# Splitting the first group's loads between SyncE's and ScalarE's DMA queues, and moving the constants and weights behind ScalarE's half

## The chip, the cores and the metric

The kernel runs on one core of one Trainium2 chip. The metric is device time in microseconds (us) from start to end of one execution; lower is better. A core has TensorE (PE, the matrix engine), VectorE (DVE), ScalarE (ACT), GpSimd (POOL) and SyncE (SP, which here only issues transfers), and 16 DMA engines that all its transfers share. An engine issues a transfer by an instruction of its own; a transfer adds 16 to a semaphore when it has landed.

## The reference

`x` is (32, 128, 56, 56) in float32. It is normalised over groups of 4 channels, whitened over groups of 8 channels with the inverse square root of their covariance, scaled, shifted and added back.

```python
def _zca_forward(x, weight, bias, groups=16):      # N, C, H, W = x.shape, c = C // groups
    xc = xf - mu                                    # per channel, over N*H*W
    xg = xc.reshape(G, c, M)
    cov = jnp.einsum('gim,gjm->gij', xg, xg) / M + EPS * jnp.eye(c)
    e, v = jnp.linalg.eigh(cov)
    proj = jnp.einsum('gik,gk,gjk->gij', v, jax.lax.rsqrt(e), v)
    xw = jnp.einsum('gij,gjm->gim', proj, xg).reshape(C, M)
    return xw * weight + bias                       # back in N, C, H, W
out = x + _zca_forward(_gn(x), L0_conv_weight, L0_conv_bias)
```

## The kernel before

**Tiling.** The 128 channels are 16 groups of 8. A group `g` of all 32 samples is two tiles (`s` = 0, 1) of 128 partitions (16 samples by 8 channels) by 3136 pixels, 1.6 MB each. Tiles live in `ring`, which holds 7 groups. A tile is loaded in two halves (`q`) of 1568 pixels, each half by four transfers of 32 partitions, 196 KB each: 16 transfers a group. `x_landed[g % 7][s][q]` counts the four of a half.

**Order.** Every engine walks the same loop of ticks (64 a group) and does what tables such as `BN_AT` say is due in that tick, for several groups in turn; the order on an engine is fixed, and semaphores join the engines. The loads of groups 1 to 6 stand before SP's loop; those of groups 7 and up wait for the store of the group that had their place.

**A group's way.** DVE takes statistics of each tile in seven chunks of 448 pixels (`row_stats`, L338): chunk 0 waits for half 0 and chunk 3 for half 1. After the 14th chunk come `rows` (L344), matmuls with constants from `cst` and small DVE steps (`deviations`, `var_eps`, `scales`, `centre`, L349 to L385), which yield `y_mul` and `y_add`. POOL and ACT then normalise the tile in pieces (L314, L499), split each into a high and a low half-precision part (ACT L511, POOL L322), DVE transposes them (L395) and PE sums their products (`ps_gram`). A chain of small matrix products gives the inverse root, and PE applies it (`ps_apply`), ACT writes the result over the tile (L520) and SP stores it.

**Start.** SP issues the 16 transfers of group 0 (tile 0 half 0, tile 0 half 1, tile 1 half 0, tile 1 half 1), then three transfers on `const_landed`: `cst` (128 x 760 floats, 380 KB) and the two rows of `wb8`, weight and bias, each gathered as 8 x 16 single floats, then groups 1 to 6. PE's first work waits for all three (`const_landed` at 48): a matmul that spreads the weights over 128 partitions (`wb_product`). DVE reads it in `read_weights` (L451 to L455), which in its fixed order stands after the 14 chunks of group 0 and ahead of `rows(0)` and of everything later. In names of the profile `wb8` and `wb` are both `wb`.

Of the kernel before, what the change touches and what calls it, by code (L numbers as in the profile page):

```python
# [15 lines left out]
CG = 8  # L16
GROUPS = C // CG
GN = 4
TILES = N * CG // P
# [6 lines left out]
RING = 7  # L26
# [19 lines left out]
PAIRS = CG // 2  # L46
HALVES = 2
HALF = HW // HALVES
# [87 lines left out]
def zca_residual(nc: bass.Bass, x: bass.AP, weight: bass.AP, bias: bass.AP, const: bass.AP, out: bass.AP):  # L136
    with ExitStack() as ctx:
        def sb(name, shape, dt=F32):
            return ctx.enter_context(nc.sbuf_tensor(name, shape, dt))
# [4 lines left out]
        def sem(name):  # L144
            return ctx.enter_context(nc.semaphore(name))

        ring = sb("ring", [P, RING, TILES, HW])
        hl_ring = sb("hl_ring", [P, HL_RING, PIECE_MAX, 2], F16)
        t_ring = sb("t_ring", [P, T_RING, PIECE_MAX, 2], F16)
        cst = sb("cst", [P, CONST_COLS])  # L150
        wb8 = sb("wb8", [CG, 2, GROUPS])
# [33 lines left out]
        x_landed = [[[sem(f"x_landed_{r}_{s}_{q}") for q in range(HALVES)] for s in range(TILES)]  # L185
                    for r in range(RING)]
        out_stored = [[sem(f"out_stored_{r}_{s}") for s in range(TILES)] for r in range(RING)]
        const_landed = sem("const_landed")
# [23 lines left out]
        x_dram = x.rearrange("(s n) (g c) h w -> g s n c (h w)", s=TILES, c=CG)  # L212
# [30 lines left out]
        def span(p):  # L243

            s, q = divmod(p, len(PIECE_UNITS))
            lo, hi = PIECE_UNITS[q]
            return s, slice(lo * UNIT, hi * UNIT)

        def width(p):
            lo, hi = PIECE_UNITS[p % len(PIECE_UNITS)]  # L250
            return (hi - lo) * UNIT
# [5 lines left out]
        def due(places, t):  # L257

            items = places.items() if isinstance(places, dict) else enumerate(places)
            return [((t - a) // TICKS, k) for k, a in items  # L260
                    if (t - a) % TICKS == 0 and 0 <= (t - a) // TICKS < GROUPS]

        def due_one(place, t):
            return [g for g, _ in due([place], t)]

        ticks = range(FIRST_TICK, LAST_TICK + 1)
        block = ctx.enter_context(nc.Block())

        @block.sync
        def _(sp):  # L270
            def load(g, s):
                r = g % RING
                if g >= RING:
                    sp.wait_ge(out_stored[r][s], 16 * PAIRS * (g // RING))
                for q in range(HALVES):
                    px = slice(q * HALF, (q + 1) * HALF)
                    for a in range(PAIRS):
                        sp.dma_start(ring[a::PAIRS, r, s, px], x_dram[g, s][:, a::PAIRS, px]).then_inc(  # L278
                            x_landed[r][s][q], 16)

            def store(g, s):
                r = g % RING
                sp.wait_ge(out_ready, PARTS * g + PARTS // TILES * (s + 1))
                for a in range(PAIRS):
                    sp.dma_start(out_dram[g, s][:, a::PAIRS, :], ring[a::PAIRS, r, s, :]).then_inc(
                        out_stored[r][s], 16)

            for s in range(TILES):
                load(0, s)
            sp.dma_start(cst[:], const).then_inc(const_landed, 16)  # L290
            with nc.allow_non_contiguous_dma(reason="256 channel scalars, once"):
                sp.dma_start(wb8[:, 0, :], weight.rearrange("(g j) o -> j (g o)", j=CG)).then_inc(const_landed, 16)
                sp.dma_start(wb8[:, 1, :], bias.rearrange("(g j) o -> j (g o)", j=CG)).then_inc(const_landed, 16)
            for g in range(1, RING):
                for s in range(TILES):
                    load(g, s)
            for t in ticks:
                for g, s in due(LOAD_AT, t):
                    if g >= RING:
                        load(g, s)  # L300
                for g, s in due(STORE_AT, t):
                    store(g, s)
            for r in range(RING):
                for s in range(TILES):
                    sp.wait_ge(out_stored[r][s], 16 * PAIRS * len(range(r, GROUPS, RING)))
# [182 lines left out]
        @block.scalar  # L488
        def _(act):
            def stats_root(g):  # L490
                act.wait_ge(stat_step, STAT_OPS * g + VAREPS)
                nc.scalar.activation(root[:], vareps, ACT.Sqrt).then_inc(root_done, 1)  # L492

            def normalise(g, p):
                s, px = span(p)
                act.wait_ge(stat_step, STAT_OPS * g + Y_SET)
                y = ring[:, g % RING, s, px]
                i = g % STAT_RING
                nc.scalar.activation(y, y, ACT.Identity, bias=y_add[:, i, s:s + 1],  # L499
                                     scale=y_mul[:, i, s:s + 1]).then_inc(y_act_ready, 1)  # L500

            def high_part(g, p):
                s, px = span(p)
                i = PIECES * g + p
                if p in Y_POOL:
                    act.wait_ge(y_pool_ready, len(Y_POOL) * g + sorted(Y_POOL).index(p) + 1)
                else:
                    act.wait_ge(y_act_ready, len(Y_ACT) * g + sorted(Y_ACT).index(p) + 1)
                if i >= HL_RING:
                    act.wait_ge(t_ready, i - HL_RING + 1)  # L510
                nc.scalar.copy(hl_ring[:, i % HL_RING, 0:width(p), 1], ring[:, g % RING, s, px]).then_inc(h_ready, 1)  # L511

            def finish(g, u):
                s, q = divmod(u, PARTS // TILES)
                if u == 0:
                    act.wait_ge(stat_step, STAT_OPS * (g + 1))
                i = PARTS * g + u
                act.wait_ge(applied, i + 1)
                px = slice(2 * BANK * q, 2 * BANK * (q + 1))
                nc.scalar.activation(ring[:, g % RING, s, px].rearrange("p (a b) -> p a b", a=2),  # L520
                                     ps_apply[:, i % 2 * 2:i % 2 * 2 + 2, 0:BANK],
                                     ACT.Identity, bias=fin_add[:, g % STAT_RING, s:s + 1],
                                     scale=scale[:, g % STAT_RING, s:s + 1]).then_inc(out_ready, 1)

            def read_hop(g, k):
                e = g % 2

                def copy(dst, src):
                    act.wait_ge(solve_mm[e], HOPS * (g // 2) + k + 1)
                    nc.scalar.copy(dst, src).then_inc(solve_read[e], 1)  # L530

                if k in HOP_WV[:-1]:
                    copy(wv[:, e], s_wv[e])
                if k == HOP_WV[-1]:
                    copy(zz[:, e], s_z[e])
                if k == HOP_T:
                    copy(tz[:, e], s_t[e])
                if k == HOP_V:
                    act.wait_ge(res_copied, g + 1)
                    copy(zx[:, e], s_zx[e])  # L540

            for t in ticks:
                for g, k in due(HOP_READ_AT, t):
                    read_hop(g, k)
                for g in due_one(ROOT_AT, t):
                    stats_root(g)
                for g, u in due(FINISH_AT, t):
                    finish(g, u)
                for g, p in due(Y_ACT, t):
                    normalise(g, p)  # L550
                for g, p in due(H_AT, t):
                    high_part(g, p)
# [122 lines left out]
```

## Time and profile before

| | |
|---|---|
| median of 3 runs | 403.22 us (402.53 to 403.56) |
| profiled execution | 402.31 us |
| its span, first to last instruction | 400.5 us |
| TensorE granted clock, mean | 0.994 |
| busy PE / DVE / ACT / POOL | 85% / 79% / 78% / 72% |
| moved by DMA | 103.72 MB, mean 259 GB/s |

The span is 1.8 us shorter than the time of the same execution; what lies around it is not in the trace. A row of the timeline gives the start, the length, the engine, line, operation and names, and how long the engine was idle before it and what ended that. A row of DMA issues gives the time in which the issuing engine was busy with them, not that of the transfer. PEld is PE's weight load.

### The profile page before, as it was taken

The page shows a single profiled execution, that of the slowest core. Times are in us where ns is not written, and L with a number is a line of the kernel's source. Part 1 is how long each engine was busy: PE and PEld are TensorE (multiplying, and loading weights), DVE is VectorE, ACT ScalarE, POOL GpSimd, SP SyncE. Part 2 cuts the span into 40 slices and gives each one's busy share as a digit, 9 for nine tenths or more (in the row PEclk, how much of TensorE's full clock was granted, in tenths as well). Part 3 has the DMA queues.
Part 4 walks back from the last instruction along what each step waited for, and adds up shares of the span by engine and source line. Part 5 has one row for each costly group of instructions (what it writes and reads, how often), then busy time and mean ns, then how long its engine had stood idle before and what let it go on. Part 6 is the DMA issues. An engine that isn't in the chain of part 4 may idle for free.

```text
span 400.5 us, 8571 instructions
## 1 busy us (share of the span) xinstructions
PE 339.3 (85%) x3202; PEld 214.2 (53%) x3202; DVE 314.5 (79%) x869; ACT 313.8 (78%) x449; POOL 287.9 (72%) x148
## 2 busy tenths in 40 slices
PE   0114366999999999999999999999999999998891
PEld 0013345666656566656565666565656666554450
DVE  2679999899999999999999999999999984531100
ACT  1065565689999999999999999898989898954572
POOL 0059979978888888889898888888888888820000
PEclk9999999999999999999999999999999999999997
DMA  7999999923999999999999999988993535354667
GB/s 224 278 305 293 295 285 291 291 50 142 292 318 314 320 306 313 304 298 316 313 300 297 297 309 315 301 281 292 319 321 121 181 118 180 124 200 160 211 204 279
DMA packets 18890, 103.72 MB, mean 259 GB/s; under 512 B 6432, under 2 KB 6432, under 8 KB 14752
## 3 DMA queue, kind: packets, MB, share of 16 engines
q1 hardware_dynamic: 18848, 103.18, 80.3%
q8 instruction: 25, 0.41, 0.4%
q14 instruction: 17, 0.14, 0.1%
HBM read 51.77 MB, written 51.38 MB: 258 GB/s over the span
## 4 chain that ended last, share of the span: by engine, by line
PE 80%; DVE 8%; POOL 4%; SPq 3%; issue 2%; ACT 1%; DMA 1%; DVEq 0%
PE ps_apply L557 48%; PE ps_small L557 15%; PE ps_gram L557 13%; PE ps_stat L557 4%; POOL hl_ring L322 3%; DVE bn L338 3%; DVE t_ring L395 3%; SPq L278 2%; DMA wb<-in_L_conv_bias_dram 1%; DVE spread_in L405 1%; ACT tz L530 1%; POOL ring L314 1%; DVE pp L424 0%; ACT hl_ring L511 0%; ACT ring L520 0%
## 5 line engine op out<-in xcount | busy, mean ns | idle before, releaser
L322 POOL TENSOR_TENSOR hl_ring<-ring,hl_ring 128x1024 f16<-128x1024 f32 (+1 forms) x96 | 230.8, 2415 | 41.2 <-ACT hl_ring L511 41.2
L557 PE MATMUL ps_apply<-ring,a_t 128*128 128x392 f32 x512 | 202.2, 520 | 0.0
L520 ACT ACTIVATE ring<-ps_apply,fin_add,scale 128x784 f32<-128x784 f32 x128 | 127.4, 995 | 16.6 <-PE ps_apply L557 16.5
L338 DVE BATCH_NORM_STATS2 bn<-ring 128x6 f32<-128x448 f32 x224 | 128.9, 602 | 8.8 <-DMA ring<-in_x_dram 8.8
L511 ACT CAST hl_ring<-ring 128x1024 f16<-128x1024 f32 (+1 forms) x96 | 129.1, 1371 | 6.7 <-POOL ring L314 3.6
L395 DVE STREAM_TRANSPOSE t_ring<-hl_ring 128x1024 f32<-128x1024 f32 (+1 forms) x96 | 119.2, 1242 | 2.9 <-POOL hl_ring L322 2.8
L557 PEld LDWEIGHTS ps_apply<-ring,a_t 128*128 128x128 f32 x512 | 87.3, 190 | 43.3 <-ACT ring L520 2.7
L557 PE MATMUL ps_gram<-t_ring 128*128 128x64 f16 x1568 | 68.5, 200 | 10.8 <-DVE t_ring L395 10.8
L314 POOL TENSOR_SCALAR ring<-ring,y_mul,y_add 128x1024 f32<-128x1024 f32 (+1 forms) x48 | 57.9, 1212 | 23.5 <-DVE y_add L382 23.5
L499 ACT ACTIVATE ring<-ring,y_add,y_mul 128x1024 f32<-128x1024 f32 (+1 forms) x48 | 59.9, 1249 | 7.9 <-DVE y_add L382 7.9
L557 PEld LDWEIGHTS ps_gram<-t_ring 128*128 128x128 f16 x1568 | 58.2, 102 | 14.0 <-DVE t_ring L395 11.3
L424 DVE SCALAR_TENSOR_TENSOR pp<-ps_small,cst 16x16 f32<-16x16 f32 x112 | 17.2, 154 | 39.3 <-PE ps_small L557 38.0
L557 PEld LDWEIGHTS ps_small<-wv 16*16 16x16 f32 x224 | 12.0, 90 | 46.6 <-issue 35.2
L530 ACT COPY wv<-ps_small 16x32 f32<-16x32 f32 x112 | 18.2, 163 | 17.5 <-PE ps_small L557 17.3
L557 PE MATMUL ps_small<-pp,wv 16*16 16x16 f32 (+1 forms) x224 | 23.5, 178 | 3.0 <-DVE pp L424 3.0
L557 PE MATMUL ps_small<-wv 16*16 16x16 f32 x224 | 23.7, 179 | 2.3 <-ACT wv L530 2.3
L557 PE MATMUL ps_small<-wv,pp 16*16 16x16 f32 x192 | 18.9, 172 | 0.0
L492 ACT ACTIVATE root<-ps_stat 128x2 f32<-128x2 f32 x16 | 2.4, 150 | 19.4 <-DVE ps_stat L360 19.3
L557 PEld LDWEIGHTS ps_small<-pp,wv 16*16 16x16 f32 (+1 forms) x224 | 11.8, 89 | 9.3 <-DVE pp L424 4.1
L557 PEld LDWEIGHTS ps_stat<-dr,cst 128*128 128x128 f32 x64 | 10.6, 216 | 8.8 <-DVE dr L377 5.2
L557 PE MATMUL ps_small<-wb,cst 8*128 8x32 f32 x2 | 0.6, 407 | 17.0 <-DMA wb<-in_L_conv_bias_dram 17.0
L557 PE MATMUL ps_stat<-dr,cst 128*128 128x1 f32 x64 | 9.6, 253 | 4.8 <-DVE dr L377 4.8
(59 smaller groups left out, 199.7 us busy)
## 6 DMA issues: line engine op xcount, KB each, us to landing
ring<-in_x_dram SPq DMA_DIRECT2D x256, 196.0 KB, 4.3
out_dram<-ring SPq DMA_DIRECT2D x128, 392.0 KB, 4.9
cst<-const_dram SPq DMA_DIRECT2D x1, 380.0 KB
wb<-in_L_conv_weight_dram SPq DMA_DIRECT2D x1, 0.5 KB
wb<-in_L_conv_bias_dram SPq DMA_DIRECT2D x1, 0.5 KB
```

The source lines that it names most:

```text
L278: sp.dma_start(ring[a::PAIRS, r, s, px], x_dram[g, s][:, a::PAIRS, px]).then_inc(x_landed[r][s][q], 16)
L314: nc.gpsimd.tensor_scalar(y, y, y_mul[:, i, s:s + 1], y_add[:, i, s:s + 1], ALU.mult, ALU.add).then_inc(y_pool_ready, 1)
L322: nc.gpsimd.tensor_tensor(hl[:, :, 0], ring[:, g % RING, s, px], hl[:, :, 1], ALU.subtract).then_inc(l_ready, 1)
L338: nc.vector.bn_stats(bn[:, g % 2, s, c, :], ring[:, g % RING, s, c * BN:(c + 1) * BN]).then_inc(bn_done, 1)
L395: nc.vector.transpose(words(t_ring[:, i % T_RING, 0:n]), words(hl_ring[:, i % HL_RING, 0:n])).then_inc(t_ready, 1)
L405: nc.vector.tensor_scalar(spread_in[:, g % 2, s], id8w[:, g], y_mul[:, g % STAT_RING, s:s + 1], None, ALU.mult)
L424: nc.vector.scalar_tensor_tensor(out=pp[:, e], in0=s_m[e], scalar=POLY[it][1], in1=ai[:, CW * it:CW * (it + 1)], op0=ALU.mult, op1=ALU.add ...
L499: nc.scalar.activation(y, y, ACT.Identity, bias=y_add[:, i, s:s + 1], scale=y_mul[:, i, s:s + 1]).then_inc(y_act_ready, 1)
L511: nc.scalar.copy(hl_ring[:, i % HL_RING, 0:width(p), 1], ring[:, g % RING, s, px]).then_inc(h_ready, 1)
L520: nc.scalar.activation(ring[:, g % RING, s, px].rearrange("p (a b) -> p a b", a=2), ps_apply[:, i % 2 * 2:i % 2 * 2 + 2, 0:BANK], ACT.Iden ...
L530: nc.scalar.copy(dst, src).then_inc(solve_read[e], 1)
L557: return nc.tensor.matmul(out_, lhsT, rhs, start=start, stop=stop, skip_group_check=True)
```

## The change

A helper `half_load` issues the four transfers of one half of a tile on the engine that it is given. `load` uses it, so that groups 1 and up are issued as before. For group 0, SP now issues half 0 of both tiles, and goes on with group 1. ACT, ahead of its loop, issues half 1 of both tiles, then `cst`, weight and bias. Semaphores, destinations and waits are the same.

```diff
+        def half_load(engine, g, s, q):
+            px = slice(q * HALF, (q + 1) * HALF)
+            for a in range(PAIRS):
+                engine.dma_start(ring[a::PAIRS, g % RING, s, px], x_dram[g, s][:, a::PAIRS, px]).then_inc(
+                    x_landed[g % RING][s][q], 16)
...
             for s in range(TILES):
-                load(0, s)
-            sp.dma_start(cst[:], const).then_inc(const_landed, 16)
-            with nc.allow_non_contiguous_dma(reason="256 channel scalars, once"):
-                sp.dma_start(wb8[:, 0, :], weight.rearrange("(g j) o -> j (g o)", j=CG)).then_inc(const_landed, 16)
-                sp.dma_start(wb8[:, 1, :], bias.rearrange("(g j) o -> j (g o)", j=CG)).then_inc(const_landed, 16)
+                half_load(sp, 0, s, 0)
             for g in range(1, RING):
...
+            for s in range(TILES):
+                half_load(act, 0, s, 1)
+            act.dma_start(cst[:], const).then_inc(const_landed, 16)
+            with nc.allow_non_contiguous_dma(reason="256 channel scalars, once"):
+                act.dma_start(wb8[:, 0, :], weight.rearrange("(g j) o -> j (g o)", j=CG)).then_inc(const_landed, 16)
+                act.dma_start(wb8[:, 1, :], bias.rearrange("(g j) o -> j (g o)", j=CG)).then_inc(const_landed, 16)
             for t in ticks:
```

What SP issues at the start of the program, before (L278 is a transfer of `x`):

```order
L278 DMA ring<-in_x_dram 32x1x1568 x16
L290 DMA cst<-const_dram 128x760
L292 DMA wb<-in_L_conv_weight_dram 8x16x1
L293 DMA wb<-in_L_conv_bias_dram 8x16x1
L278 DMA ring<-in_x_dram 32x1x1568 x96
```

The same place on SP in the changed kernel, where a transfer of `x` is L269 and a store L288:

```order
L269 DMA ring<-in_x_dram 32x1x1568 x104
L288 DMA out_dram<-ring 16x2x3136 x8
L269 DMA ring<-in_x_dram 32x1x1568 x8
L288 DMA out_dram<-ring 16x2x3136 x4
L269 DMA ring<-in_x_dram 32x1x1568 x8
```

Eight of the first 16 transfers and the three small ones are gone from SP, so that the first of group 1 is its ninth.

ACT's first instructions before:

```order
L492 ACT_TABLE_LOAD
L492 ACTIVATE root<-ps_stat 128x2
L499 ACTIVATE ring<-ring,y_add,y_mul 128x1024
L511 CAST hl_ring<-ring 128x1088
L511 CAST hl_ring<-ring 128x1024 x2
```

ACT's first instructions in the changed kernel:

```order
L269 DMA ring<-in_x_dram 32x1x1568 x8
L543 DMA cst<-const_dram 128x760
L545 DMA wb<-in_L_conv_weight_dram 8x16x1
L546 DMA wb<-in_L_conv_bias_dram 8x16x1
L491 ACT_TABLE_LOAD
L491 ACTIVATE root<-ps_stat 128x2
L498 ACTIVATE ring<-ring,y_add,y_mul 128x1024
L510 CAST hl_ring<-ring 128x1088
```

The eleven transfers stand ahead of the table load, which was ACT's first instruction.

## Rows read from the trace of the kernel before

**Rows 1.** The page: the chain that ended last, shares of the span.
```profile
PE 80%; DVE 8%; POOL 4%; SPq 3%; issue 2%; ACT 1%; DMA 1%; DVEq 0%
PE ps_apply L557 48%; PE ps_small L557 15%; PE ps_gram L557 13%; PE ps_stat L557 4%; POOL hl_ring L322 3%; DVE bn L338 3%; DVE t_ring L395 3%; SPq L278 2%; DMA wb<-in_L_conv_bias_dram 1%; DVE spread_in L405 1%; ACT tz L530 1%; POOL ring L314 1%; DVE pp L424 0%; ACT hl_ring L511 0%; ACT ring L520 0%
```

**Rows 2.** The chain in order of time, first 20 us: start, length, what.
```profile
11.61 0.37 SPq L292
11.99 0.04 issue
12.03 4.92 DMA wb<-in_L_conv_bias_dram
16.94 0.04 issue
16.99 0.65 PE ps_small L557 x2
17.63 0.02 issue
17.66 0.17 DVE wb L451
```

**Rows 3.** Timeline of DVE, first 30 us.
```profile
6.08 1.68 DVE L338 BATCH_NORM_STATS2 bn<-ring 128x6 f32<-128x448 f32 x3 [5.12 <-DMA ring<-in_x_dram]
9.22 2.21 DVE L338 BATCH_NORM_STATS2 bn<-ring 128x6 f32<-128x448 f32 x4 [1.47 <-DMA ring<-in_x_dram]
11.82 1.68 DVE L338 BATCH_NORM_STATS2 bn<-ring 128x6 f32<-128x448 f32 x3 [0.40 <-DMA ring<-in_x_dram]
15.29 2.20 DVE L338 BATCH_NORM_STATS2 bn<-ring 128x6 f32<-128x448 f32 x4 [1.79 <-DMA ring<-in_x_dram]
17.66 0.17 DVE L451 TENSOR_SCALAR wb<-ps_small 128x16 f32<-128x16 f32 x1 [0.16 <-PE ps_small L557]
...
19.90 1.14 DVE L338 BATCH_NORM_STATS2 bn<-ring 128x6 f32<-128x448 f32 x2
```

**Rows 4.** Timeline of SP's queue, first 50 us.
```profile
0.74 10.20 SPq L278 DMA_DIRECT2D ring<-in_x_dram  x16
10.98 0.59 SPq L290 DMA_DIRECT2D cst<-const_dram  x1
11.61 0.37 SPq L292 DMA_DIRECT2D wb<-in_L_conv_weight_dram  x1
12.03 0.28 SPq L293 DMA_DIRECT2D wb<-in_L_conv_bias_dram  x1
12.35 37.51 SPq L278 DMA_DIRECT2D ring<-in_x_dram  x58
```

**Rows 5.** Windows: stretch and length, busy by engine (count), PEclk, DMA share, GB/s.
```profile
2.00:3.00 1.00, 0.00 (x0) 0.00 (x0) 0.00 (x0) 0.01 (x1) 0.00 (x0) 1.00 0.72 207
...
13.00:14.00 1.00, 0.00 (x0) 0.00 (x0) 0.50 (x1) 0.00 (x0) 0.00 (x0) 1.00 0.89 203
14.00:15.00 1.00, 0.00 (x0) 0.00 (x0) 0.00 (x0) 0.00 (x0) 0.00 (x0) 1.00 0.99 221
15.00:16.00 1.00, 0.00 (x0) 0.00 (x0) 0.71 (x2) 0.00 (x0) 0.00 (x0) 1.00 0.75 179
16.00:17.00 1.00, 0.01 (x1) 0.01 (x1) 1.00 (x3) 0.00 (x0) 0.00 (x0) 1.00 0.94 364
```

**Rows 6.** Windows of longer stretches, same columns.
```profile
18.00:28.00 10.00, 2.16 (x8) 1.93 (x8) 7.85 (x27) 4.22 (x5) 3.75 (x3) 1.00 1.03 304
28.00:60.00 32.00, 14.33 (x191) 12.30 (x191) 30.44 (x63) 19.35 (x21) 28.97 (x15) 1.00 1.03 292
...
80.00:100.00 20.00, 19.75 (x200) 12.52 (x199) 18.50 (x53) 18.57 (x27) 15.99 (x9) 1.00 0.30 97
```

**Rows 7.** The page: DMA packets of the whole run, and issues with KB each.
```profile
DMA packets 18890, 103.72 MB, mean 259 GB/s; under 512 B 6432, under 2 KB 6432, under 8 KB 14752
...
ring<-in_x_dram SPq DMA_DIRECT2D x256, 196.0 KB, 4.3
out_dram<-ring SPq DMA_DIRECT2D x128, 392.0 KB, 4.9
cst<-const_dram SPq DMA_DIRECT2D x1, 380.0 KB
wb<-in_L_conv_weight_dram SPq DMA_DIRECT2D x1, 0.5 KB
```

**Rows 8.** Timeline, first 45 us: ACT's first work.
```profile
0.73 1.28 ACT L492 ACT_TABLE_LOAD   x1 [0.73 <-PEq L660]
...
21.14 0.17 ACT L492 ACTIVATE root<-ps_stat 128x2 f32<-128x2 f32 x1 [19.13 <-DVE ps_stat L360]
```

**Rows 9.** Waits of the whole run: who waited for whom, us, times, longest.
```profile
DVE bn L338 <- DMA ring<-in_x_dram: 8.8, 4, 5.1
```

More of the change, by code:

```diff
@@ L275, in load @@
                 for q in range(HALVES):
[L276 to L279, printed above, removed]
+                    half_load(sp, g, s, q)
             def store(g, s):
```

## The prediction

> **What bounds the kernel now.** I read the chain of the page first: PE holds 80% of it, and at its head stand transfers issued by SP and the landing of the bias [rows 1]. The chain in order of time shows that head: SP issues until 12.03, the bias lands 4.92 us later at 16.94, PE spreads the weights, and DVE reads them at 17.66 [rows 2]. DVE's timeline shows how close a second chain runs: the four halves of group 0 are taken up at 6.08, 9.22, 11.82 and 15.29, the last four chunks take 2.20 us, and DVE then idles only 0.16 us for the weights [rows 3]. Two things therefore set 17.66: the 14 chunks, done at 17.49, and the bias at 16.94. Both must come earlier if anything is to be won, and either alone delays everything, because all later DVE work, group 1's chunks at 19.90 among it [rows 3], stands behind the reading of the weights.
>
> Is the stream of transfers or the issuing the limit at the start? SP takes 10.20 us for 16 issues, or 0.64 us each with the gap to the next [rows 4]. With a full backlog the core moves 304 GB/s [rows 6], so a transfer of 196 KB (200,704 bytes, [rows 7]) takes 0.66 us. The stream is the limit from the start, by a hair. Data flows at 207 GB/s in the first window, so it began about 2.3 [rows 5]. Sixteen transfers need 2.3 + 16 x 0.66 = 12.9. The first four land at 6.08 where 2.3 + 4 x 0.66 is 4.9, so landing lags by 1.1: the sixteenth could land at 14.0. It did at 15.29, in the stretch from 13 to 16, where only 203, 221 and 179 GB/s moved [rows 5]. That is where cst and the single floats of weight and bias go through.
>
> A shift at the head is a shift of the end. DVE waits for loads four times in all, 8.8 us [rows 9], and those are the four waits of group 0 [rows 3]; behind it DVE is busy 30.44 of 32 us, then PE 19.75 of 20 [rows 6]. No later wait for a load is there to absorb or give back time. I count one for one.
>
> **The change, part by part.**
>
> *Eight issues off SP.* Together SP and ACT issue group 0 by 0.74 + 8 x 0.64 = 5.9 instead of 10.98 [rows 4]. The stream does not go faster for it, since it was the limit. SP goes on with group 1 at 5.9, so two backlogs share the DMA engines from then on. If they alternate evenly, ACT's eighth transfer is the sixteenth served, and lands at 14.0.
>
> *Order of landing.* Both halves of tile 0 now fill together: half 0 is served seventh, half 1 eighth (2.3 + 8 x 0.66 + 1.1 = 8.7). Tile 1's half 0 is the fifteenth and lands at 13.3. DVE then has all seven chunks left, at 0.55 us each (2.20 / 4): 13.3 + 3.9 = 17.2, against 17.49. So the statistics gain 0.3 us at most; what was an overlap of chunks with the last half is given up. An uneven share, ACT's issues being slower, say, only moves the sixteenth later.
>
> *cst, weight and bias on ACT's queue.* They are issued at 5.9 to 7.2 instead of 10.98 to 12.3, but stand behind ACT's half and beside SP's backlog. Alone on the stream they took from 14.0 (the sixteenth's due landing) to 16.94: 2.9 us. New is what SP's queue sends between them. The trace has no second busy queue, so this price must be bounded. From below: ACT's small transfers are served at once, 0, and the bias lands at 14.0 + 2.9 = 16.9, as before. From above: each packet of theirs lets one whole packet of x pass.
>
> The page tells how many packets they are. 6432 packets are under 512 B [rows 7]: the 256 single floats, and 6176 others, which is 385 x 16 + 2 x 8: one completion for each engine and transfer, with weight and bias on 8 engines only. So on each of those 8 engines cst is 8 rows and a completion, and weight and bias are 16 floats and a completion each: 9 + 17 + 17 = 43 packets. A transfer of x is three packets an engine (2 rows of 6272 B, a completion) in 0.66 us, 0.22 us a packet on average. If the engines alternate packet by packet, 43 x 0.22 = 9.5 us go in between. The bias lands at 14.0 + 2.9 + 9.5 = 26.4. With 0.33 for each (only rows of x counted) it would be 14.2, and with cst shared by bytes and no turn for it, 34 x 0.22 = 7.5. I take 9.5, since the profile counts single floats and completions as packets of their own, and a packet is the nearest thing in the trace to a unit of turns.
>
> The Trainium skill's page "DMA: Bandwidth & Descriptors", section "Queues, rings and completion order", says that SP's and ACT's queues are two rings on each of the same engines, served in turn, a whole packet at a time, and that a packet typically holds 9 to 17 descriptors. No row here shows turns. If the 17 entries of weight on an engine were one such packet, the engine would go through them in one turn, which is the first rival below.
>
> *ACT.* Eleven issues at 0.64 and less put the table load from 0.73 to about 7.2, and its 1.28 us end by 8.5; ACT's first work is at 21.14 [rows 8]. Nothing else is queued there. Cost nothing; the cover is 12 us.
>
> *The sum.* DVE reads the weights at 26.4 + 0.7 (PE's matmuls and the hand-over, 16.94 to 17.66, [rows 2]) = 27.1 instead of 17.66: +9.5. The statistics, done by 17.2, wait. Against the profiled execution, 402.31 + 9.5 = 411.8; the median of the runs is 0.9 above that execution, so 412.7. A gain from group 1 having landed meanwhile isn't there: its chunks did not wait before.
>
> **The rivals.** Measurement of this kernel can tell about 0.3%, 1.2 us, from no change.
>
> *Turns of whole transfers, or order of arrival.* cst, weight and bias each let one transfer of x pass: 3 x 0.66 = 2.0. By arrival it is about the same, as SP has issued three of group 1 by the time that ACT has issued the bias. Bias at 18.9, +2.0, 405.2. For it: it is the simplest way for an engine to share, and the skill's packet of many descriptors gives it. Against it: the packets of the profile are single rows and floats.
>
> *No change.* Either ACT's small transfers are hardly held up, or the two issuers hold each other up so that SP gets no head start (issues at 1.3 us each, and the order of before in effect; the change would then not do what it says). DVE is bound by the chunks at 17.2 to 17.5: within 1.2 us of 403.2.
>
> *Faster.* Two queues on each engine lift the stream. For one microsecond after the dip it ran at 364 GB/s [rows 5]. At that rate a transfer takes 0.55: the sixteenth lands at 2.3 + 8.8 + 1.1 = 12.2, the fifteenth at 11.7, chunks end at 15.5, and the bias, if not held up, comes at 12.2 + 2.9 = 15.1 and is read at 15.8: -1.9, 401.3. It decides only if the bias lands before 15.7; with even one transfer of x let past for each of the three, it lands at 16.7 and nothing is won. Against it speaks the flat 304 and 292 GB/s with a deep backlog [rows 6]. The same page of the Trainium skill, section "Issuing engines are not separate DMA queues", says that issuing on several engines saves only issue time; the 304 GB/s agrees so far as one queue can show it.
>
> **How the numbers follow.** Packet-wise turns 0.45 (its own range 410 to 417, from 7.5 and 14.2); turns of whole transfers 0.30 (404.4 to 407); between these two or beyond by another sharing 0.05; no change 0.14; faster 0.06. The likeliest gives 412.7. From 404.3 to 416.0 the range leaves out no change, faster, and the far end of the first. Faster 0.06, same 0.14, slower 0.80.
>
> **What the profile after would show.** DVE's waits: both halves of tile 0 near 8.7 with one long wait, tile 1 near 13.3. If the step on the turns is right, PE's first matmul starts near 26.5 and DVE's L451 idles some 9 us, released by PE; with whole transfers it starts near 19. The windows from 14 to 26 should then stay near 300 GB/s without the dip. ACT's table load is near 7. Everything after L451 keeps its distances. The prediction is wrong if the first matmul starts before 17.5, if the halves of group 0 land much before 13, or if a later wait on POOL or PE swallows the delay.

## The result, and the profile after

The changed kernel takes 411.64 us (median of 4 runs, 409.7 to 414.2), the kernel before 403.12 (402.53 to 403.56): 1.0216 times as long, 95% interval 1.0154 to 1.0278. Slower, as forecast: the medians are 8.5 us apart, where 9.5 were forecast, and the whole interval lies above 1. The profiled execution took 412.55 us with a span of 410.7, 10.2 more than before. Its traffic is split over two queues now. From the page of the profile: queue and kind, then packets, MB and the share of the 16 engines' time.

```profile
q1 hardware_dynamic: 18048, 101.18, 75.2%
q10 hardware_dynamic: 800, 2.00, 1.7%
```

q10 is ACT's: 8 transfers of x, cst, weight and bias. The chain of the page names the new wait, against 1% in [rows 1]:

```profile
PE ps_apply L562 48%; PE ps_small L562 15%; PE ps_gram L562 12%; DMA wb<-in_L_conv_bias_dram 4%; PE ps_stat L562 4%; POOL hl_ring L321 3%; DVE bn L337 3%; DVE t_ring L394 3%; ACTq L269 1%; DVE spread_in L404 1%; ACT tz L529 1%; POOL ring L313 1%; DVE pp L423 0%; ACT hl_ring L510 0%; ACT ring L519 0%
```

In order of time, the same chain (before: [rows 2]):

```profile
5.99 0.60 ACTq L543
6.63 0.81 ACTq L545
7.47 17.38 DMA wb<-in_L_conv_bias_dram
24.90 0.65 PE ps_small L562 x2
25.57 0.18 DVE wb L450
```

The bias was issued at 7.47 instead of 12.03 and landed 17.4 us later instead of 4.9. The timeline shows both queues and DVE (before: [rows 3, 4, 8]):

```profile
0.74 34.77 SPq L269 DMA_DIRECT2D ring<-in_x_dram  x54
0.75 5.21 ACTq L269 DMA_DIRECT2D ring<-in_x_dram  x8
...
7.79 1.28 ACT L491 ACT_TABLE_LOAD   x1 [7.79 <-issue]
9.84 3.79 DVE L337 BATCH_NORM_STATS2 bn<-ring 128x6 f32<-128x448 f32 x7 [8.88 <-DMA ring<-in_x_dram]
14.67 3.79 DVE L337 BATCH_NORM_STATS2 bn<-ring 128x6 f32<-128x448 f32 x7 [1.05 <-DMA ring<-in_x_dram]
...
25.57 0.18 DVE L450 TENSOR_SCALAR wb<-ps_small 128x16 f32<-128x16 f32 x1 [7.11 <-PE ps_small L562]
```

The four waits for x became two, the chunks of a tile run in one piece of seven, and DVE, done with all 14 at 18.46, then stands still for 7.11 us. Meanwhile the stream is full, with x of group 1 and later (columns as in [rows 5]):

```profile
18.00:20.00 2.00, 0.00 (x0) 0.00 (x0) 0.46 (x1) 0.00 (x0) 0.00 (x0) 1.00 1.00 311
20.00:22.00 2.00, 0.00 (x0) 0.00 (x0) 0.00 (x0) 0.00 (x0) 0.00 (x0) 1.00 1.04 326
22.00:24.00 2.00, 0.00 (x0) 0.00 (x0) 0.00 (x0) 0.00 (x0) 0.00 (x0) 1.00 1.07 339
```

**Where the 10.2 us went.** L450 is 7.9 us late (25.57 against 17.66), and the first `ps_apply` matmul just as late: 83.57 against 75.64. The rest arises there. First the kernel before, then the changed one, PE's timeline:

```profile
75.64 2.98 PE L557 MATMUL ps_apply<-ring,a_t 128*128 128x392 f32 x4
...
79.20 1.58 PE L557 MATMUL ps_apply<-ring,a_t 128*128 128x392 f32 x4
```

```profile
83.57 2.98 PE L562 MATMUL ps_apply<-ring,a_t 128*128 128x392 f32 x4
...
87.37 2.98 PE L562 MATMUL ps_apply<-ring,a_t 128*128 128x392 f32 x4
...
91.39 1.58 PE L562 MATMUL ps_apply<-ring,a_t 128*128 128x392 f32 x4
```

Four matmuls take 2.98 us at first and 1.58 later, which I read as TensorE at the lower of its two clocks (1.2 GHz) and then at the higher (2.4 GHz); the section on the clock shows why. Before, one set of four ran at the lower clock, after, two. From the first `ps_apply` to the 33rd it was 22.0 us before and 23.9 after (22.02 and 23.85). From there to the last `ps_apply` the two kernels keep their distance to 0.1 us. So: 7.9 for the bias, 1.8 for the clock, 0.1 on the way, and 0.4 behind the last `ps_apply`. Those 0.4 are not the change's: the trace of before has 8.8 us there, and every other trace below, kernels with an early start among them, has 9.1 to 9.2.

### The profile page after: what moved, and what is told of

Its sections match the earlier page's. It is cut to its first block, busy times and chain, and to the rows that moved or that the text cites. A ratio compares the mean times of both kernels' runs of the same rounds, so it can differ in the third digit from the quotient of the medians.

```text
span 410.7 us, 8571 instructions
## 1 busy us (share of the span) xinstructions
PE 341.2 (83%) x3202; PEld 215.2 (52%) x3202; DVE 314.6 (77%) x869; ACT 313.7 (76%) x449; POOL 288.2 (70%) x148
## 4 chain that ended last, share of the span: by engine, by line
PE 78%; DVE 8%; DMA 4%; POOL 4%; ACTq 2%; issue 1%; ACT 1%; DVEq 0%
PE ps_apply L562 48%; PE ps_small L562 15%; PE ps_gram L562 12%; DMA wb<-in_L_conv_bias_dram 4%; PE ps_stat L562 4%; POOL hl_ring L321 3%; DVE bn L337 3%; DVE t_ring L394 3%; ACTq L269 1%; DVE spread_in L404 1%; ACT tz L529 1%; POOL ring L313 1%; DVE pp L423 0%; ACT hl_ring L510 0%; ACT ring L519 0%
## 5 line engine op out<-in xcount | busy, mean ns | idle before, releaser
L519 ACT ACTIVATE ring<-ps_apply,fin_add,scale 128x784 f32<-128x784 f32 x128 | 127.5, 996 | 16.5 <-PE ps_apply L562 16.4
L423 DVE SCALAR_TENSOR_TENSOR pp<-ps_small,cst 16x16 f32<-16x16 f32 x112 | 17.2, 154 | 40.9 <-PE ps_small L562 39.5
L562 PE MATMUL ps_small<-wb,cst 8*128 8x32 f32 x2 | 0.6, 407 | 24.9 <-DMA wb<-in_L_conv_bias_dram 24.9
```

The source lines that it names most:

```text
L423: nc.vector.scalar_tensor_tensor(out=pp[:, e], in0=s_m[e], scalar=POLY[it][1], in1=ai[:, CW * it:CW * (it + 1)], op0=ALU.mult, op1=ALU.add ...
L562: return nc.tensor.matmul(out_, lhsT, rhs, start=start, stop=stop, skip_group_check=True)
```

## The experiments

The kernel before was run beside them again: 404.56 (25 runs), 403.77 (16) and 404.55 (19) in three sessions, in a spread of some 402 to 405.7. Each kernel's ratio is against its own session. "L451" is DVE's reading of the weights, whatever its line in that kernel.

### The change once more

> The changed kernel once more, for a second trace. Packet-wise turns: PE's first matmul again starts at 24.9 (within 1 us), DVE idles some 7 us ahead of L450, and the head is 7.9 us late. In the first trace another 1.8 us were lost between 80 and 90 us, where the first eight ps_apply matmuls took about 0.74 us each against 0.40 later (before: four such). If that loss hangs on the moment at which TensorE goes from 1.2 to 2.4 GHz, it will differ in this trace while the head stays at 7.9. Rival: the spread of the changed kernel's times (409.7 to 414.2) comes from the landing of the bias; then PE's first matmul moves by microseconds.

411.71 us (410.23 to 413.84), ratio 1.0181, interval 1.0134 to 1.0229. Timeline of DVE and PE:

```profile
14.93 3.79 DVE L337 BATCH_NORM_STATS2 bn<-ring 128x6 f32<-128x448 f32 x7 [1.74 <-DMA ring<-in_x_dram]
25.96 0.50 PEld L562 LDWEIGHTS ps_small<-wb,cst 8*128 8x128 f32 x2 [25.96 <-DMA wb<-in_L_conv_bias_dram]
```

Both expectations hold in part: the first matmul moved by 1.1 us (24.90, 25.96), just beyond the 1 us that I had allowed, and the loss at the clock is there again with 24.1 us from the first to the 33rd `ps_apply`. So the landing of the bias is one source of the changed kernel's spread: it makes 1.1 of the 1.3 us between its two profiled executions. That the clock is a second one is not shown for this kernel, since both its traces have the long piece; other kernels below differ there.

### x split, small transfers on SP

```diff
             for s in range(TILES):
                 half_load(sp, 0, s, 0)
+            sp.dma_start(cst[:], const).then_inc(const_landed, 16)
+            with nc.allow_non_contiguous_dma(reason="256 channel scalars, once"):
+                sp.dma_start(wb8[:, 0, :], weight.rearrange("(g j) o -> j (g o)", j=CG)).then_inc(const_landed, 16)
+                sp.dma_start(wb8[:, 1, :], bias.rearrange("(g j) o -> j (g o)", j=CG)).then_inc(const_landed, 16)
...
             for s in range(TILES):
                 half_load(act, 0, s, 1)
-            act.dma_start(cst[:], const).then_inc(const_landed, 16)
...
```

> Half of the change: x of group 0 split over SP and ACT, but cst, weight and bias behind SP's half and ahead of its group 1. Packet-wise turns: ACT's queue is empty by then, nothing goes between the 43 packets, and the bias lands by 17; the chunks, which end at 18.5 as in the changed kernel since tile 1 lands near 14.7 and leaves seven, set L451: 0.8 us later than before, about 404.0. Rival (two busy queues are themselves the cost): first matmul stays beyond 20 and the time near 411.

403.74 us, ratio 0.9998, interval 0.9972 to 1.0024: the loss is gone. Timeline:

```profile
9.86 3.78 DVE L341 BATCH_NORM_STATS2 bn<-ring 128x6 f32<-128x448 f32 x7 [8.90 <-DMA ring<-in_x_dram]
15.07 3.79 DVE L341 BATCH_NORM_STATS2 bn<-ring 128x6 f32<-128x448 f32 x7 [1.43 <-DMA ring<-in_x_dram]
16.70 0.50 PEld L562 LDWEIGHTS ps_small<-wb,cst 8*128 8x128 f32 x2 [16.70 <-DMA wb<-in_L_conv_bias_dram]
...
18.77 0.16 DVE L454 TENSOR_SCALAR wb<-ps_small 128x16 f32<-128x16 f32 x1
```

The bias is there at 16.70, though two queues carried x as in the change. The chunks set L451 at 18.77, 1.1 us later than before: splitting x gains nothing, it costs a microsecond of overlap. That microsecond is too small for the times to show.

### x on SP as before, small transfers on ACT

```diff
-            sp.dma_start(cst[:], const).then_inc(const_landed, 16)
...
+            act.dma_start(cst[:], const).then_inc(const_landed, 16)
+            with nc.allow_non_contiguous_dma(reason="256 channel scalars, once"):
+                act.dma_start(wb8[:, 0, :], weight.rearrange("(g j) o -> j (g o)", j=CG)).then_inc(const_landed, 16)
+                act.dma_start(wb8[:, 1, :], bias.rearrange("(g j) o -> j (g o)", j=CG)).then_inc(const_landed, 16)
             for t in ticks:
```

> The other half: all 16 transfers of x on SP as before, only cst, weight and bias on ACT, first thing. Packet-wise turns: cst's 9 and the 34 packets of weight and bias each let one of SP's pass, so the bias lands near 13 although it is issued by 2.2. Whole-transfer turns: it lands near 7. In both the 380 KB of cst now go ahead of part of x: the last half lands near 16.3, the chunks end near 18.5, L451 is 0.9 us late, about 404.1. If small packets cost the x stream nothing, 403.1.

403.31 us, ratio 0.9975, interval 0.9944 to 1.0005. Timeline:

```profile
0.74 0.38 ACTq L538 DMA_DIRECT2D cst<-const_dram  x1
1.15 0.79 ACTq L540 DMA_DIRECT2D wb<-in_L_conv_weight_dram  x1
1.97 0.28 ACTq L541 DMA_DIRECT2D wb<-in_L_conv_bias_dram  x1
...
6.99 0.49 PEld L557 LDWEIGHTS ps_small<-wb,cst 8*128 8x128 f32 x2 [6.99 <-DMA wb<-in_L_conv_bias_dram]
...
15.56 2.21 DVE L334 BATCH_NORM_STATS2 bn<-ring 128x6 f32<-128x448 f32 x4 [1.04 <-DMA ring<-in_x_dram]
17.69 0.15 DVE L447 TENSOR_SCALAR wb<-ps_small 128x16 f32<-128x16 f32 x1
```

A miss for packet-wise turns as I had worked them out: the bias landed at 6.99, not 13, and near 7 is what the whole-transfer rival had. By itself this run speaks for that rival; the three experiments below speak against it. The packet records of this trace allow another reading. SP's first packet of x starts at 2.98 us. All 128 floats of weight start between 3.5 and 4.0, when SP had issued five transfers; the bias's start between 4.3 and 6.4 and take 2 us. So the same 128 floats took 0.5 us and then 2, beside the same stream. I read it like this: a turn costs something only if the other queue has a packet waiting, and SP, which issues hardly faster than the stream drains, has next to no backlog in the first microseconds. The sum would have needed that condition; where the change issues them, at 6 to 7.5, two engines have issued at twice the pace and SP is ahead. The records do not show how full a queue is, so this condition is argued and not shown. Moving cst forward cost x little: the last half landed at 15.56 against 15.29, though 380 KB went ahead of it, and the stream has no dip like that of [rows 5] from 13 to 16 us.

### The change, weight and bias as 16 rows of 8 floats

```diff
-                act.dma_start(wb8[:, 0, :], weight.rearrange("(g j) o -> j (g o)", j=CG)).then_inc(const_landed, 16)
-                act.dma_start(wb8[:, 1, :], bias.rearrange("(g j) o -> j (g o)", j=CG)).then_inc(const_landed, 16)
+            act.dma_start(wb16[:, 0, :], weight.rearrange("(g j) o -> g (j o)", j=CG)).then_inc(const_landed, 16)
+            act.dma_start(wb16[:, 1, :], bias.rearrange("(g j) o -> g (j o)", j=CG)).then_inc(const_landed, 16)
+            act.wait_ge(const_landed, 48)
+            nc.scalar.copy(wbt[:].rearrange("p a (n c) -> p a n c", c=CG),
+                           wb16[:].unsqueeze(2).broadcast_to([GROUPS, 2, SAMPLES, CG])).then_inc(wb_tiled, 1)
```

PE then multiplies `wbt` with a 16 x 16 identity.

> The whole change, but weight and bias each come as 16 rows of 8 floats (32 bytes), one row an engine, 2 packets an engine and transfer with the completion instead of 17; ACT spreads them to 128 columns with one copy and PE multiplies with an identity (6 KB more of constants). Packet-wise turns: 13 packets instead of 43 on an engine; cst landed by 17.3 in the changed kernel's trace, two small transfers add about 1, the copy 0.3, so L451 near 19.3, 1.6 us later than before: 404.8. Whole-transfer turns, or the wait being one for bytes or for the order of issue: still three transfers, nothing gained, 411.6.

405.56 us, ratio 1.0054, interval 1.0025 to 1.0084. Timeline:

```profile
18.69 0.40 ACT L550 COPY wbt<-wb 16x256 f32<-16x256 f32 x1 [9.82 <-DMA wb<-in_L_conv_bias_dram]
...
20.21 0.17 DVE L453 TENSOR_SCALAR wb<-ps_small 128x16 f32<-128x16 f32 x1 [1.54 <-PE ps_small L567]
```

The same bytes of weight and bias, the same number of transfers, the same queue and place; weight and bias each go over all 16 engines instead of 8, and the packets on the busiest engines are 13 instead of 43. The bias lands at 18.7 instead of 24.9 to 26.0. Of the rivals only turns by packet give that. L451 is 0.9 later than I had worked out: from the landing on, the copy and PE's two products took 1.5 us, where I had 1.0, and the bias itself came 0.4 later.

### One more gather of 128 floats

```diff
+                act.dma_start(wb8_again[:], weight.rearrange("(g j) o -> j (g o)", j=CG)).then_inc(const_landed, 16)
                 act.dma_start(wb8[:, 0, :], weight.rearrange("(g j) o -> j (g o)", j=CG)).then_inc(const_landed, 16)
...
-            pe.wait_ge(const_landed, 48)
+            pe.wait_ge(const_landed, 64)
```

> The whole change with one more gather of weight (128 single floats, to a spare tile) ahead of it on ACT's queue, and PE waits for it too: 17 packets more on each of 8 engines. Packet-wise turns at the 0.22 us that the last traces show: 3.7 us more, PE's first matmul at 28.6 to 29.7 (24.9 and 26.0 in two traces of the change), time 415.4 within 2. Whole-transfer turns, or a fixed delay of the second queue: at most 0.7 us more, 412.

414.96 us, ratio 1.0301, interval 1.0254 to 1.0348: 11.2 us above the kernel before of its session, where the change was 7.2 above that of its own. Timeline:

```profile
28.25 0.63 PE L564 MATMUL ps_small<-wb,cst 8*128 8x32 f32 x2 [28.25 <-DMA wb<-in_L_conv_bias_dram]
```

The first matmul starts 0.35 us ahead of the 28.6 to 29.7 expected. In this trace the last completions of cst and of the three gathers are 17.4, 21.0, 24.7 and 28.2 us: 3.6, 3.7 and 3.5 for 17 packets each, 0.21 a packet. In the first trace of the change, cst and the two gathers end at 17.5, 21.3 and 24.9, in the second at 17.9, 22.1 and 25.9. The price of a turn goes with the rate of the stream: from 18 to 24 us it was 320, 325 and 294 GB/s in these three traces, in this order, and a gather took 3.6, 3.7 and 4.0 us. Most of the 1.1 us between the two traces of the change is that.

The packet records show the turns themselves. In the first trace of the change, in each microsecond from 17 to 23, ACT's queue starts 36 to 41 packets, and SP's queue 71 to 81 (rows and completions). The records do not name the engine; with ACT's on the 8 engines of the prediction and SP's spread evenly over 16, that is 4.5 to 5.1 an engine against 4.4 to 5.1: one for one.

### The change, SP's group 1 held back

```diff
+            sp.wait_ge(const_landed, 48)
             for g in range(1, RING):
```

> The whole change, but SP waits until cst, weight and bias have landed and only then issues group 1: nothing is left that can go between their packets. Packet-wise turns: bias lands by 17, as before the change, and the chunks (end 18.5) set L451 near 18.8; group 1, issued from 17 on, has its first half down near 22, so its first chunk waits about 1 us: 405.5 within 1.5. If the slow landing came from ACT's queue itself, first matmul stays near 25 and the time is 412 or more, with group 1 late on top.

406.05 us, ratio 1.0054, interval 1.0026 to 1.0083. Timelines of PE and DVE:

```profile
16.41 0.63 PE L563 MATMUL ps_small<-wb,cst 8*128 8x32 f32 x2 [16.41 <-DMA wb<-in_L_conv_bias_dram]
```

```profile
18.87 0.15 DVE L451 TENSOR_SCALAR wb<-ps_small 128x16 f32<-128x16 f32 x1
...
21.63 1.15 DVE L338 BATCH_NORM_STATS2 bn<-ring 128x6 f32<-128x448 f32 x2 [0.46 <-DMA ring<-in_x_dram]
...
24.98 0.63 DVE L338 BATCH_NORM_STATS2 bn<-ring 128x6 f32<-128x448 f32 x1 [0.70 <-DMA ring<-in_x_dram]
```

Nothing about ACT's queue was touched, and the bias lands 8.5 us earlier. What held it were SP's packets of group 1. The price of holding them back shows too: two short waits for group 1, 0.46 and 0.70 us.

### TensorE's clock

Every trace gives the same 58.0 us (57.9 to 58.0) from L451 to the first `ps_apply` where nothing in between was changed, but for 58.6 where group 1 was held back, and 294.1 us from the 33rd to the last. What varies is the piece between, with the start of the clock record:

| kernel | first `ps_apply` | clock record starts, after it | first to 33rd |
|---|---|---|---|
| before | 75.6 | 2.9 | 22.0 |
| change | 83.6 | 7.3 | 23.9 |
| change again | 84.6 | 8.1 | 24.1 |
| split, small on SP | 76.7 | 3.7 | 22.2 |
| small on ACT | 75.6 | 8.5 | 24.3 |
| change, rows | 78.2 | 3.2 | 22.1 |
| weight twice | 86.9 | 3.1 | 22.0 |
| group 1 held | 77.5 | 3.2 | 22.1 |

So the 1.8 us of the changed kernel's first trace do not come with a late start as such: "small on ACT", with L451 where it was before, has the long piece too, and the latest kernel (weight twice, 86.9) has the short one. Both traces of the change have the long piece, though, and two are too few to say that it always has. The runs of one kernel fall apart in the same way: the ten of "split, small on SP" are six from 403.0 to 404.0 and four from 405.25 to 405.95. Three kernels tried to move the rise. The first does each of group 1's blocks in `gram` twice:

```diff
+                if g == 1:
+                    for b in list(range(units)):
+                        pair = t_ring[:, i % T_RING, b * UNIT:(b + 1) * UNIT]
+                        product(ps_apply[:, 3, 0:UNIT], pair.rearrange("p c k -> p (c k)"), pair[:, :, 1])
```

> The kernel before, with group 1's six blocks of ps_gram matmuls done twice, the first time into a spare bank (100 matmuls more between 52 and 67 us, PE busier ahead of its first ps_apply). In six traces so far the clock record of TensorE starts between 2.9 and 8.5 us after the first ps_apply, and the time from the first to the 33rd ps_apply is 22.0 to 24.3 us in step with it. If that rise is the lottery, a rise ahead of the first ps_apply makes it about 21 and the time 401.5 to 402.5, less what the doubled blocks (6 x 1.0 us at the lower clock) delay the chain of small products, 0 to 3 us. If the rise doesn't come earlier, 403 to 408.

406.57 us, ratio 1.0073, interval 1.0045 to 1.0102. In the trace the rise came 8.1 us after the first `ps_apply`, as late as ever, and the doubled blocks delayed that to 77.64, 60.0 us after L451 instead of 58.0. In this execution doubling them did not bring the rise forward. That it never does is not shown: the mean granted clock was 0.993 or 0.994 in four of the seven runs, the traced one among them, but 0.976, 0.976 and 0.986 in the other three, and in the traces below such a lower mean stands for a rise ahead of `ps_apply` that is lost again. No trace of those three runs was kept, and at 404.85, 406.3 and 406.94 they are not clearly faster. The other two do idle products of constants; the lines for `g == 1` are in the second of them only:

```diff
+            def idle_work(n, cols=BANK):
+                for _ in range(n):
+                    product(ps_apply[:, 3, 0:cols], k_("bmask"), cst[:, 0:cols])
...
+                if (g, p) == (0, PIECES - 1):
+                    idle_work(1)
+                if g == 1:
+                    idle_work(1, BANK // 2)
...
+                if (g, k) == (0, 0):
+                    idle_work(3)
```

> The kernel before, with four idle products (128 x 392 floats, constants times constants into a spare bank; 1.5 us each at the lower clock) where PE waits anyway: one ahead of group 0's last ps_gram block (2.2 us of waiting at 42.6) and three ahead of its first small product (4.1 us at 45.9). In all traces so far the clock record starts only after wide ps_apply matmuls have run. If such work raises the clock wherever it stands, the record starts near 47 to 50, and if it holds until 75.6, the first to the 33rd ps_apply takes about 21 instead of 22.0 to 24.3: 401 to 402.5, always. If it falls again before the first ps_apply, as before the change with 0.4 us at most for the third product: 402.5 to 405.5.

> The same, and one half-size idle product (0.75 us at the lower clock, 0.4 at the higher) ahead of each of group 1's six ps_gram blocks, to keep the clock up until the first ps_apply at 75.6. If the clock of the run before rises and falls back, it holds here: 401 to 402.5. If it never rises that early, the six products delay the chain of small products by 1 to 3 us: 404 to 408. If it holds in the other kernel too, this one is the same or up to 1 us slower than that.

404.36 us, ratio 0.9997 (0.9971 to 1.0023), and 406.19, ratio 1.0053 (1.0027 to 1.008). PE's timeline of the first kernel, then of the second, has the same three idle products (six matmul records) at two paces, and the first half-size product:

```profile
46.40 4.05 PE L557 MATMUL ps_apply<-cst 128*128 128x392 f32 x6
```

```profile
44.90 2.22 PE L557 MATMUL ps_apply<-cst 128*128 128x392 f32 x6
...
52.23 1.02 PE L557 MATMUL ps_apply<-cst 128*128 128x196 f32 x2
```

Windows of the first of the two (columns as in [rows 5]):

```profile
45.00:50.00 5.00, 4.45 (x22) 2.68 (x22) 4.91 (x6) 2.98 (x3) 4.65 (x3) 1.00 1.03 279
50.00:55.00 5.00, 2.42 (x37) 1.48 (x35) 5.00 (x13) 1.37 (x2) 3.94 (x3) 0.85 1.03 281
55.00:60.00 5.00, 3.89 (x49) 3.33 (x49) 5.00 (x14) 4.86 (x8) 3.39 (x2) 0.50 1.02 280
...
76.00:80.00 4.00, 4.00 (x18) 2.08 (x15) 2.54 (x8) 2.13 (x3) 4.00 (x2) 0.50 1.02 281
80.00:86.00 6.00, 6.00 (x38) 3.51 (x37) 4.59 (x13) 3.44 (x6) 2.99 (x2) 0.65 0.79 226
```

The clock record of the first kernel starts at 50.1, at the end of the three idle products, and that of the second at 44.1, behind the single one; the three then took 2.22 us instead of 4.05, so the clock did rise there. It was back at 0.50 from 53.5 and 50.9 us, after PE had waited and done small products. It rose anew at 84.2 and 85.1, and the piece from the first to the 33rd `ps_apply` was 24.1 in both. The half-size products came too late for their purpose: the first stands at 52.23, behind the fall. They had no raised clock to hold, did not raise it again, and cost 1.9 us of chain. Whether they would hold a raised clock is open. So the clock can be raised early, but here it was lost again before it was wanted.

These two kernels also tie the two kinds of runs to the clock. As their clock record starts early, a later second rise lowers the mean granted clock of a run. In the first, three runs have 0.959 or 0.960 and take 402.5 to 403.0 us, seven have 0.955 or 0.956 and take 404.0 to 405.5. In the second, three have 0.960 or 0.961 and take 404.4 to 404.8, seven have 0.951 to 0.955 and take 406.0 to 407.2. Nothing here beats the kernel before beyond its interval; the nearest is "small on ACT" at 0.9975 (0.9944 to 1.0005).

## Why the prediction was right, point by point

*What bounds the start.* Right. The head is one for one: L451 7.9 us late, the first `ps_apply` 7.9 late, and the same 58.0 between them. That everything after L451 would keep its distances was too much: from the first `ps_apply` to the 33rd there are 1.8 us more, for the clock.

*The stream, not the issuing, is the limit.* Right. Both issuers were done with group 0 by some 6 us and the statistics were not done earlier (18.46 against 17.49). But the landings were forecast too early: half 0 of tile 0 and of tile 1 were expected so that DVE starts at 8.7 and 13.3, and it started at 9.84 and 14.67; the chunks ended at 18.5, not 17.2. The term that fails is "2.3 + n x 0.66 + 1.1": with both queues in use (the change 9.84 and 14.67, split, small on SP 9.86 and 15.07) the last of the four transfers of a half lands about a microsecond later than that sum, and why is open. It cost nothing in the changed kernel, where the bias was later still, but with it "no change" should have been forecast at 404.2 instead of 403.2.

*Turns by packet.* Right, and now shown: fewer packets with the same bytes (18.7), more packets (28.2), and no packets of the other queue (16.4) move the landing as 0.21 to 0.24 us a packet has it. "Small on ACT" missed its number; the condition that I had left out, a backlog on the other queue, would explain that.

*The size.* 26.4 was expected for the bias, 24.9 and 26.0 came. The cst part fits: 14.0 + 1.3 (380 KB at 304 GB/s) + 9 x 0.22 = 17.3, and its last completion is at 17.5 in the changed kernel's first trace. The floats are over-counted: I gave them 34 x 0.22 for the packets between and kept, in the 2.9, the 1.6 us that they took by themselves before. In that trace a gather takes 3.6 to 3.7 us for its 17 packets in all, so that their own time adds nothing beside the packets of x: 17.5 + 34 x 0.22 is 25.0.

*Packets and queues.* The Trainium skill's page "DMA: Bandwidth & Descriptors", section "Queues, rings and completion order", has the engines go round between queues a packet at a time, which these traces bear out. Its typical 9 to 17 descriptors a packet don't fit here: the gather with 17 entries an engine did not pass in one turn or two, but in 3.5 to 4.1 us, one turn for each float. The measurement decides: for these transfers a packet is a single row, float or completion. The Trainium skill's section "Issuing engines are not separate DMA queues" says that a second issuing engine saves only issue time. These runs agree: from 18 to 24 us, with both queues busy, the change moved 325 and 294 GB/s in its two traces, and from 28 to 38, with SP's alone, 330 and 306. The change lost time all the same, by the order in which things land.

*The total.* 412.7 was forecast and 411.64 measured. That it came so near is in part luck. The landing of the bias was over-estimated by 0.4 to 1.5 us. TensorE's clock, which the prediction did not know of, added 1.8 and 2.1 us in the two traces of the change against that of before; the granted clock showed 1.00 from the start there, and I took that for the clock. The 0.9 us from the profiled execution to the median went the other way: the profiled execution of the change took 412.55 us, 0.9 above its median. And the four runs of before beside it were all of the shorter kind; against the 25 of the next session the change costs 7.2 us (411.71 and 404.56).

## What to carry to other kernels

Beside another queue with a backlog, the landing of a small transfer goes by its packets and not by its bytes: each lets one packet of the neighbour pass, so that a gather of 128 floats beside a stream of 6 KB rows took 3.5 to 4.1 us. Put small transfers that something waits for on the queue of the stream itself, ahead of what may wait (16.70 here), or issue them before that queue has a backlog (6.99); and gather in rows (18.7 instead of 24.9). A second issuer pays if issuing is the limit, and at 0.64 us a transfer against 0.66 us of stream it was not.

## What the runs showed of the hardware that was not expected

TensorE's granted clock reads 1.00 until its first record, which need not be true: in the trace of before, whose record starts at 78.5 us, four `ps_apply` matmuls took 2.98 us ahead of it and 1.58 behind it, and in the kernels with idle work, which have a record earlier, four that took 2.98 stand in a stretch that reads 0.50. In every trace the rise that lasted came 2.9 to 8.5 us after the first `ps_apply`. It differs between traces, and in the two kernels with idle work the mean clock parts the runs into two kinds some 2 us apart. The runs of before fall apart likewise, 11 from 402.49 to 403.40 and 14 from 404.51 to 405.72, and a few runs of a kernel can all be of one kind, as the first four of before were (402.53 to 403.56).
